# The stage between the two attentions of a transformer block: another form for the quotients, other engines for the norms, another order of iterations

## The reference

```python
h = layernorm(x) * (1 + ca) + sa                    # ca, sa, ga, cb, sb, gb: from a small conditioning product
x = x + ga * favor_attention(h)                     # 16 heads of 16, 64 random features each
    # phiQ, phiK = exp features; KV = phiK^T V; Ksum = sum(phiK)
    # out = (phiQ KV) / (phiQ Ksum + 1e-6);  out @ Wo^T + bo
h = layernorm(x) * (1 + cb) + sb
x = x + gb * expert_attention(h)
    # chunk e of 512 tokens: layernorm again, with norm_w and norm_b; only its first 256 >> e columns count
    # q, k, v = xm W^T + b; softmax(q k^T / 16) v with 8 heads over all 2048 tokens
    # output product over the first 256 >> e columns, + o_b, + h
```

## Time and profile before

| | us |
|---|---|
| three runs | 2006.68 to 2007.88, median 2007.24 |
| the profiled execution | 2007.16, its span 2005.4 |
| L842 to the first score, first batch | 188.56 to 308.34 |
| TensorE busy, share of the span | 1750.5, 87% |
| VectorE | 1450.5, 72% |
| ScalarE | 1083.1, 54% |
| GpSimd | 1179.5, 59% |
| mean granted clock of TensorE | 0.934 |

### The profile page before, as it was taken

How to read it: one execution, slowest core, us unless ns; L and a number is a source line. 1 busy time by engine, 2 the same in 40 slices (tenths; PEclk the granted TensorE clock), 3 DMA queues, 4 the chain that set the end, 5 groups by cost and what they waited for, 6 DMA issues and landing times.

```text
span 2005.4 us, 31471 instructions
## 1 busy us (share of the span) xinstructions
PE 1750.5 (87%) x11520; PEld 997.9 (50%) x11520; DVE 1450.5 (72%) x2617; ACT 1083.1 (54%) x1998; POOL 1179.5 (59%) x974
## 2 busy tenths in 40 slices
PE   5698869999899886999979977799997988599997
PEld 3576434444377543444447744344435764344443
DVE  4686777777478577777648857777766876787774
ACT  0586333656578432566648823266665863336564
POOL 0685354666768346566768723666676853546666
PEclk8898978999999897999989989899998989889999
DMA  4000043001110025101020003500111000430011
GB/s 126 1 2 1 18 158 85 17 11 39 53 33 2 1 72 167 30 9 48 1 85 2 2 1 117 140 12 17 41 34 52 2 2 0 171 89 16 12 37 43
DMA packets 55714, 87.56 MB, mean 44 GB/s; under 512 B 13188, under 2 KB 32004, under 8 KB 52868
## 3 DMA queue, kind: packets, MB, share of 16 engines
q1 hardware_dynamic: 55560, 85.54, 14.5%
HBM read 49.68 MB, written 35.70 MB: 43 GB/s over the span
## 4 chain that ended last, share of the span: by engine, by line
PE 65%; DVE 14%; ACT 10%; issue 4%; POOL 3%; DMA 2%; SPq 2%; POOLq 0%; ACTq 0%; DVEq 0%
PE PS L1175 12%; PE PS L1300 11%; PE PS L1288 9%; PE PS L1313 5%; PE PS L1069 5%; DVE MXP L861 4%; PE PS L1096 3%; PE PS L1077 3%; PE PS L1218 3%; PE PS L1106 3%; ACT HT L525 2%; ACT HTR L528 2%; PE PS L1245 2%; DVE QKS L911 2%; ACT PHIQ L563 2%
## 5 line engine op out<-in xcount | busy, mean ns | idle before, releaser
L498 POOL TENSOR_TENSOR TS<-PR 128x1024 f32<-128x1024 f32 (+1 forms) x256 | 573.1, 2239 | 336.7 <-ACT PR L664 336.7
L861 DVE TENSOR_REDUCE MXP<-PS 128x1 f32<-128x512 f32 x960 | 598.0, 680 | 202.7 <-PE PS L1175 199.3
L664 ACT ACTIVATE PR<-PS 128x512 f32<-128x512 f32 x960 | 504.8, 602 | 425.9 <-PE PS L1288 422.4
L1175 PE MATMUL PS<-KOP,QOP 96*128 96x512 f32 x960 | 422.8, 460 | 45.1 <-DMA KOP<-k_scr 34.2
L1288 PE MATMUL PS<-QOP,KOP 97*128 97x512 f32 x960 | 379.4, 409 | 18.1 <-ACT PR L664 12.7
L1175 PEld LDWEIGHTS PS<-KOP,QOP 96*128 96x128 f32 x960 | 190.7, 200 | 300.3 <-DVE MXP L861 174.7
L1300 PE MATMUL PS<-PR,V 128*32 128x512 f32 x1920 | 273.1, 606 | 0.0
L1288 PEld LDWEIGHTS PS<-QOP,KOP 97*128 97x128 f32 x960 | 181.3, 192 | 85.6 <-ACT PR L664 50.2
L445 POOL TENSOR_TENSOR RSTD<-VE,minus_half 128x4 f32<-128x4 f32 x32 | 33.9, 1060 | 237.6 <-DVE VE L758 237.6
L1313 PE MATMUL PS<-TS,ones 128*32 128x512 f32 x960 | 133.2, 593 | 5.4 <-POOL TS L498 5.4
L1069 PE MATMUL PS<-W1T,HTR 128*128 128x512 f32 x384 | 115.1, 438 | 21.2 <-POOL HTR L402 21.0
(11 more groups left out here) (144 smaller groups left out, 2691.0 us busy)
## 6 DMA issues: line engine op xcount, KB each, us to landing
KOP<-k_scr SPq DMA_DIRECT2D x84, 256.0 KB, 6.0
k_scr<-QKS SPq DMA_DIRECT2D x64, 256.0 KB, 2.8
QOP<-q_scr SPq DMA_DIRECT2D x180, 64.0 KB, 2.0
q_scr<-QKS SPq DMA_DIRECT2D x40, 256.0 KB, 2.8
X<-in_L_attn_x_dram SPq DMA_DIRECT2D x16, 512.0 KB, 4.8
out_dram<-X SPq DMA_DIRECT2D x16, 512.0 KB, 3.1
QOP<-MXT SPq DMA_DIRECT2D x240, 0.5 KB
KOP<-k_scr SPq DMA_DIRECT2D x48, 64.0 KB, 2.0
```

Source lines behind the costliest of these rows:

```text
L498: g.tensor_tensor(sums(k)[:, 0:len(stage)], pair[:, :, 0], pair[:, :, 1], ALU.add).then_inc(S["psum_t"], 1)
L664: a.activation(PR[:, k % 2, w, q], bank(score_bank(p, n, w, q)), ACT.Exp).then_inc(S["ex"], 1)
L861: v.tensor_reduce(MXP[:, u % 2, i, kc:kc + 1], bank(max_bank(p)), AX.X, ALU.max).then_inc(S["am_rd"], 1)
L1175: mm(bank(max_bank(p)), QOP[0:96, u % QS6, i * P:(i + 1) * P], KOP[0:96, h % KS6, kc * CH:(kc + 1) * CH], start=True, stop=True).then_inc( ...
```

## The change

The chunks come in the order 3, 1, 0, 2. `KVW` takes the place of `NW` and `DW`: 34 columns, 32 of KV and two of Ksum. For each tile of 128 tokens and each of the 8 groups `PHIQ` is now the stationary operand (128 columns) and `KVW` moves (34 columns), so that numerators and denominators come out with tokens as rows, in one bank for each tile, three banks in turn. VectorE adds the epsilon, takes reciprocals, and multiplies, tile by tile (`quotients`); TensorE transposes the quotients (`merge`), ScalarE copies them to `MT` (`merged`), and the projection is as before.

The centring goes to ScalarE as `Identity` with a scale and a bias for each token (`centred`, `centred_again`), for which VectorE writes the negative mean and GpSimd multiplies it (`deviations`). Scale and shift of `Hh` are VectorE's for all four chunks. `QKS`'s low part is read straight from the bank, `TMP` is gone, V is copied without its bias by ScalarE, and the bias is in `OBE`, made once in the setup by ten more matmul instructions. Banks 5 to 7 form a ring for `X2`, V, Q and K. The loop has four iterations and a tail of two chunks, and Q, K and V of a chunk come two iterations behind. The non-attention part of the result waits for the last low part, and its last chunk is made among the first slots; VectorE waits for it at slot 9. The last two `query_features` use banks 0 and 1.

```diff
-    expert = (3, 0, 1, 2)
+    expert = (3, 1, 0, 2)
...
+        BO, OBE = sb("BO", [P, D]), sb("OBE", [P, sum(width)])
-        NW, DW = sb("NW", [P, GR, 32]), sb("DW", [P, GR, 32])
+        KVW = sb("KVW", [P, GR, 34])
...
-            return p % 3 if p >= INSIDE else 4 + p % 4
+            return p % 3 if p >= INSIDE else p % 4
+        def kinds(s):
+            ks = list(range(KD if expert[s] == 0 else 1))
+            xt = [("x", s, k) for k in ks]
+            vp, qk = [("v", s, h) for h in range(2)], [("q", s, n) for n, _ in blocks(s)]
+            return xt + (vp + qk if s + 2 < NC else qk + vp)
+        order = [kind for s in range(NC) for kind in kinds(s)]
+        place = {kind: i for i, kind in enumerate(order)}
+        def ring(kind):
+            return 5 + place[kind] % 3
+        def freed(b, kind):
+            if place[kind] < 3:
+                return S["kw_ok"], 4 * (b + 1)
+            what, s, i = order[place[kind] - 3]
+            if what == "q":
+                return S["q_lo"], NQ * b + i + 1
+            if what == "v":
+                return S["v2_sb"], 2 * (NC * b + s) + i + 1
+            return S["xn_sb"], xns(b, s) + i + 1
...
+                    if s == 0:
+                        sp.wait_ge(S["nd"], NT * (b + 1))
...
+                def deviations(s, ready, signal, count):
+                    cols, n = slot(s), NC * b + s + 1
+                    wait_all(pool, (S[ready], 2 * n))
+                    g.tensor_tensor(RSTD[:, cols], VE[:, cols], minus_half[:, cols], ALU.pow).then_inc(S["rs"], 1)
+                    pool.wait_ge(S["rs"], 2 * NC * b + count)
+                    g.tensor_tensor(NMR[:, cols], NEGM[:, cols], RSTD[:, cols], ALU.mult).then_inc(S[signal], 1)
...
+                    if it >= 1:
+                        deviations(it - 1, "ve3", "nmr3", count)
                     if it < NC:
...
+                        deviations(it, "ve2", "nmr2", count)
...
+                wait_all(pool, (S["q_lo"], NQ * (b + 1)))
                 own_g(g.tensor_tensor(OWG[:], OWT[:], gate.broadcast_to([P, KD, D]), ALU.mult))
...
+                for e in results[:-1]:
+                    for step in range(3):
+                        output_base(e, step)
...
+                    if k in (1, 3, 5):
+                        output_base(results[-1], k // 2)
...
+                def centred(s):
+                    g = NC * b + s
+                    act.wait_ge(S["nmr2"], g + 1)
+                    for t in range(s * TPC, (s + 1) * TPC):
+                        a.activation(Hh[:, t], X[:, t], ACT.Identity, bias=NMR[:, t:t + 1], scale=RSTD[:, t:t + 1]
+                                     ).then_inc(S["xh2"], 1)
+                def centred_again(s):
+                    g, m = NC * b + s, D if expert[s] == 0 else P
+                    act.wait_ge(S["nmr3"], g + 1)
+                    act.wait_ge(S["x2T"], xns(b, s))
+                    for i in range(TPC):
+                        t = s * TPC + i
+                        a.activation(X2[:, i, 0:m], Hh[:, t, 0:m], ACT.Identity, bias=NMR[:, t:t + 1],
+                                     scale=RSTD[:, t:t + 1]).then_inc(S["x2"], 1)
...
+                for it in range(NC):
+                    if it >= 1:
+                        centred(it - 1)
+                    if it >= 2:
+                        normal(it - 2)
+                    merged(it, 0)
+                    if it >= 2:
+                        values_bank(it - 2, 0)
+                    merged(it, 1)
+                    if it >= 2:
+                        values_bank(it - 2, 1)
+                    if it >= 1:
+                        centred_again(it - 1)
+                    if it >= 2:
+                        high_qk(it - 2)
+                normal(NC - 2)
+                centred(NC - 1)
+                high_qk(NC - 2)
+                values_bank(NC - 2, 0)
+                values_bank(NC - 2, 1)
+                centred_again(NC - 1)
+                normal(NC - 1)
+                high_qk(NC - 1)
+                values_bank(NC - 1, 0)
+                values_bank(NC - 1, 1)
...
+                def quotients(s, h):
+                    g = NC * b + s
+                    pair = [(i, (TPC * s + i) % 3) for i in (2 * h, 2 * h + 1)]
+                    for i, at in pair:
+                        nd = bank(at)[:, 0:34 * GR].rearrange("p (g c) -> p g c", c=34)
+                        dve.wait_ge(S["nd"], TPC * g + i + 1)
+                        if TPC * g + i >= TPC:
+                            dve.wait_ge(S["m"], TPC * (g - 1) + i + 1)
+                        counted = mark(v.tensor_scalar(R[:, i], nd[:, :, 32:34], FAVOR_EPS, None, ALU.add))
+                        if i % 2 == 0:
+                            first = counted
+                    dve.wait_ge(S["dve_own"], first)
+                    first = mark(v.reciprocal(R[:, 2 * h], R[:, 2 * h]))
+                    dve.wait_ge(S["dve_own"], counted)
+                    counted = mark(v.reciprocal(R[:, 2 * h + 1], R[:, 2 * h + 1]))
...
+                    for i, at in pair:
+                        nd = bank(at)[:, 0:34 * GR].rearrange("p (g c) -> p g c", c=34)
+                        dve.wait_ge(S["dve_own"], first if i % 2 == 0 else counted)
+                        v.tensor_tensor(M[:, i].rearrange("p (g h d) -> p g h d", g=GR, h=2),
+                                        nd[:, :, 0:32].rearrange("p g (h d) -> p g h d", h=2),
+                                        R[:, i].rearrange("p g (h o) -> p g h o", o=1).broadcast_to([P, GR, 2, DK]),
+                                        ALU.mult).then_inc(S["m"], 1)
+                def second_input(s):
+                    dve.wait_ge(S["xh2"], TPC * (NC * b + s + 1))
+                    for op, m in ((ALU.mult, 2), (ALU.add, 1)):
+                        own(v.tensor_tensor(Hh[:, slot(s)], Hh[:, slot(s)],
+                                            MODB[:, bass.ds(b, 1), m, :].broadcast_to([P, TPC, D]), op))
+                    statistics(range(s * TPC, (s + 1) * TPC), [Hh[:, s * TPC + i] for i in range(TPC)], "ve3")
...
+                def low_parts(s):
+                    for n, t in blocks(s):
+                        dve.wait_ge(S["q_hi"], NQ * b + n + 1)
+                        v.scalar_tensor_tensor(QKS[:, n % 3, 1], bank(ring(("q", s, n))), qk_bias(t),
+                                               QKS[:, n % 3, 0].bitcast(F32), ALU.add, ALU.subtract
+                                               ).then_inc(S["q_lo"], 1)
+                for it in range(NC):
+                    quotients(it, 0)
+                    quotients(it, 1)
+                    if it >= 1:
+                        second_input(it - 1)
+                    residual(it)
+                    if it >= 2:
+                        low_parts(it - 2)
+                maxima(0, EARLY)
+                second_input(NC - 1)
+                low_parts(NC - 2)
+                maxima(EARLY, 2 * EARLY)
+                low_parts(NC - 1)
+                maxima(2 * EARLY, 3 * EARLY)
...
+                    if k == STEPS + 1:
+                        dve.wait_ge(S["base"], NC * (b + 1))
...
+            pe.wait_ge(S["vb_ok"], KD)
+            for e in range(EXPERTS):
...
+                for k in ks:
+                    last = mm(bank(3)[:, o:o + m], VBC[0:rows, k], OWT[0:rows, k, 0:m], start=k == 0,
+                              stop=k == len(ks) - 1)
+            last.then_inc(S["obm"], 1)
...
+                def numerators(s, i):
+                    n = TPC * s + i
+                    if n >= 3:
+                        pe.wait_ge(S["m"], NT * b + n - 2)
+                    for gr in range(GR):
+                        last = mm(bank(n % 3)[:, 34 * gr:34 * gr + 34], PHIQ[:, gr, n * P:(n + 1) * P], KVW[:, gr],
+                                  start=True, stop=True)
+                    last.then_inc(S["nd"], 1)
...
+                for i in range(3):
+                    numerators(0, i)
+                for it in range(NC):
+                    if it >= 2:
+                        second_transposes(it - 2)
+                    numerators(it, 3)
+                    merge(it, 0)
+                    if it >= 2:
+                        second_values(it - 2, 0)
+                    merge(it, 1)
+                    projected(it, 0)
+                    projected(it, 1)
+                    if it >= 2:
+                        second_values(it - 2, 1)
+                    if it < NC - 1:
+                        for i in range(3):
+                            numerators(it + 1, i)
+                    if it >= 2:
+                        second_qk(it - 2)
+                maxima(0, EARLY)
+                for s in (NC - 2, NC - 1):
+                    second_transposes(s)
+                    second_qk(s)
+                    second_values(s, 0)
+                    second_values(s, 1)
+                    maxima((s - NC + 3) * EARLY, (s - NC + 4) * EARLY)
```

(53 more changed lines are left out.)

343 lines of the change are left out of this document (99 added, 244 removed).

## The result

| | kernel before | changed kernel |
|---|---|---|
| median, same chip | 2007.24 us (2005.34 to 2008.23, 5 runs) | 2041.19 us (2035.35 to 2048.70, 5 runs) |
| ratio to before, 95% interval | 1 | 1.0172 [1.0144, 1.0199] |
| profiled execution | 2007.16 us | 2048.70 us, span 2046.9 us |

The change makes the kernel 1.7% slower, 34 us at the medians. Its profiled execution is the longest of the five, so the traces differ by 41.5 us.

The account below looks back on a forecast made before the run. Bound: the middle stage's per-chunk loop of waits and waiting tail, no engine full. Layout 302.0 plus clock 16.6 gives 318.6, 10.3 later; four batches 41.2 plus setup 3.7 add 45 to 2007.16: 2052, range 1983 to 2072.

Parts of the forecast that it names:

- The clock decides, and the numerators don't raise it: Middle stage: 34-column matmuls don't raise TensorE's clock and let it fall near a run's end; 16.6 us a batch.
- Rival (A): Middle stage: clock high from 199 on and stays; 21.5 us less, 1986; chance 20%.
- Rival (B): Clock low until the first wide projection and after the ring's gap, not falling in numerators; 8.0 a batch, 2018; chance 22%.
- (C): Tail alone sets the stage's length; two waits worse by a landing, 2.8, make Rival (B) 2029; chance 8%.
- How it starts: First four tiles of numerators in each batch run at the low clock; 3.7 us lost.
- Layout at the high clock: Middle stage, copy of sums to first score: first score at 302.0 against 308.3, gaining 6.3 us a batch.
- The clock term: Middle stage: low-clock cost of numerators, projections, merges, Q and K; 16.6 us a batch, bounds 0 and 20.
- The start: First numerators of the middle stage come 5.1 us behind the copy of the sums.
- From last low part to score: End of the middle stage: stores, loads, maxima and DMAs stay as before, about 15.8 us.
- Tail: From the last loop's merge to the end of the last low parts in the middle stage: 34.5 us.
- Setup: Once, ahead of the batches: ten more instructions and four sums, less a smaller memset; 3.7 us.
- GpSimd's work behind the low parts: Some 20 us moved ahead of GpSimd's first sums, costed at nothing; 2 to 3 us a batch if uncovered.

## Why the prediction was right

The forecast was 2052 and the median 2041.19; 45 us more were foretold and 34 measured. The profiled execution, the slowest of the five, took 2048.70. The term that the prediction called decisive decided, but its parts were missed in both directions, and that their sum came out near is partly luck.

- **The clock decides, and the numerators don't raise it**: shown. The first 64 numerator instructions run at 1.00 when they have 64 columns and at 0.58 when they have 34, and with 64 the whole kernel is 52 us faster at the medians, more than all that the change had lost. Rival (A), in which a TensorE without gaps holds the clock, fell with its 1986: it was busy 11.95 of 12.00 us at 0.58. Rival (B) fell with the falls inside the runs. (C) stood on (B)'s clock, and neither of its two waits came out a landing worse: the two parts of the tail are 1.5 and 0.3 us longer than foretold.
- **How it starts was wrong.** The sum had the first four tiles low because the stage begins low, 3.7 lost. The clock was at 1.00 from 195 on and fell 2 us into them; they took 12.14 us and not 7.36, 4.8 lost.
- **Layout at the high clock**, 113.5 us from copy to score: the 64-column kernel has 110.6 to 112.4 in its trace, with a few falls left in it. Its distances between second merges are 12.5, 12.9 and 20.9, foretold as 13.0, 13.8 and 19.7. Foretold were 6.3 a batch less than before. The traces give 7.7; the medians of the whole kernels (20 us less, with 3.9 more ahead of the first copy) give 5.9.
- **The clock term**, 16.6, upper bound 20. The step to 64 columns gives back 13 a batch at the medians and 17.8 between the two traces; the falls that are left in the 64-column kernel come on top. The parts made up for each other. The numerators lose most: by group (mean over the four batches) 41.4 us, where 256 instructions at 0.115 are 29.4, so 11.9 lost and not 7.9. The projections lose 2.2 and not 7.2: 4.27, 4.64, 4.10 and 3.62 us, since the clock returns within a projection. Q and K behind the fourth run lose 2.7, not 1.0.
- **The start** of the numerators, 5.1 behind the copy: 4.0. **From last low part to score**, 15.8: 16.1. **Tail** from the last merge to the last low part, 34.5: 36.0. **Setup**, 3.7: 3.9, and `MODB`'s products start 2.2 later.
- **GpSimd's work behind the low parts, costed at nothing**: held. Its first sum of the stage starts at 324.52, and the stage behind is no longer than before.
- **The place of the gain was right, the reason given for it wrong.** From the last transposes ahead of the last chunk's projection to the last low part the kernel before takes 50.2 us (L1229, 242.59 to 292.75) and the 64-column kernel 36.7 (252.29 to 289.01), while the way there is 5 us longer. But "no low part waits 2 us beside GpSimd any more" names a stall that was real (2 us each) and cost nothing: with it removed alone, the kernel before keeps its time to 0.1%. Its low parts ended into SyncE's queue, and with that cleared too, into a wait for queries. Which of the other edits shortens the tail was not isolated; the chunk order alone doesn't, by the run that undid it. That Q, K and V come two iterations behind and not three is the likely one, not shown.
- **The spread.** The changed kernel varies by 13 us between runs where the one before varied by 3, and the 64-column kernel by 19; the prediction had no term for that. Stages of identical work differ by 5.3 us within the changed kernel's trace, the longest at the lowest clock. Why a kernel with fewer falls spreads as much stays open.

The Trainium skill, TensorE: Matmul & The Clock Gate, section "What's actually happening", ties the gate to how busy the engine was, and says that instructions aren't counted. This trace does not agree if busy is what the profile calls busy: at equal instruction counts and an engine without a gap, 34 columns gave 0.58 and 64 gave 1.00.

## What to carry to other kernels

A stage made of narrow matmuls can be slower than its instruction count says because the clock falls under it, and it takes the wide matmuls beside it along. Padding the moving operand with zero columns, here from 34 to 64 at no cost per instruction, is a small edit to try; it held the clock in the two-instruction form and not in the single-pass one. Before a stall is put down as a gain, follow what comes next in every queue: here kernels that brought the last low part forward by 3 us or more met a transfer that was queued for another reason. Before two traces are subtracted, see where each execution lies among the runs of its kernel. If the granted clock differs between two kernels, sum the stage at both levels first and compare layouts only after that.

## What the runs showed of the hardware

- An instruction with 128 stationary columns took 0.115 us at the high clock with 32 and with 64 moving columns alike (8 in 1.07, 64 in 7.36), and 0.21 at the low one with 34.
- A busy TensorE isn't enough for the high clock: with 34-column instructions it was busy 11.95 of 12.00 us, and the granted clock fell from 1.00 to 0.50 about 2 us in; with 64 columns it stayed at 1.00 in the same place.
- The clock rose from 0.50 to 1.00 behind transposes without a gap (busy 2.60 of 2.60 us until 195.00), so here it took no 512-wide matmuls.
- Single-pass instructions cost hardly more each (24 in 2.94 us with 34 columns, 2.95 with 64) and halve their number, but left the stage's clock lower with 64 columns (0.81) than two-instruction ones of 64 columns (0.87), and the kernel was still some 27 us faster.
- A VectorE subtraction of two 128x512 tiles in SBUF took 2.04 us while GpSimd worked on tiles in SBUF, and 0.69 once GpSimd's work was moved behind it.
